# A wider slot table for the first experts, smaller last slot groups and evenly dealt scatters in a two-layer attention and experts kernel

## The reference: what is computed

```python
x = x + L0_xattn(layernorm(x), ctx, ...)   # 16 heads, masked by equal layer index
x = x + L0_ffn(layernorm(x))               # 8 experts, top 2 of each token, no capacity limit
x = x + L1_xattn(layernorm(x), ctx, ...)   # two-way attention and a gate
x = x + L1_ffn(layernorm(x))               # 8 experts, top 2, at most 640 tokens an expert

# L0_ffn
top_w, top_idx = top_k(softmax(xf @ router_w.T), 2)
combine = sum(one_hot(top_idx, E) * softmax(top_w)[..., None], axis=1)
out = einsum('te,ted->td', combine, silu(x @ w1[e]) @ w2[e] * scale[e])
# L1_ffn
seq = cumsum(expert_label, axis=0) * expert_label
valid = (seq > 0) & (seq <= capacity)
slot = seq - 1                            # where the token stands in its expert's buffer
out = (silu(disp @ W1) * (disp @ W2)) @ W3
```

## Time and profile before

| | |
|---|---|
| time, three runs | 1536.22 us median (1533.29 to 1537.31) |
| profiled execution | 1534.38 us, of it 1532.6 us from the first to the last instruction |
| PE busy | 1356.7 us (89%) |
| DVE, ACT, POOL busy | 847.2, 816.1, 671.5 us |
| mean granted TensorE clock | 0.955 of full speed |

### The profile page before, as it was taken

One profiled execution on the slowest core, in us unless ns is written; L12 is line 12 of the kernel. 1 busy time (PEld: TensorE's weight loads), 2 busy tenths in 40 slices (PEclk: granted clock), 3 DMA queues, 4 the chain that ended last, 5 costly groups with the idle time before them and its releaser, 6 DMA issues.

```text
span 1532.6 us, 37450 instructions
## 1 busy us (share of the span) xinstructions
PE 1356.7 (89%) x12922; PEld 1100.2 (72%) x12922; DVE 847.2 (55%) x2350; ACT 816.1 (53%) x1904; POOL 671.5 (44%) x935
## 2 busy tenths in 40 slices
PE   5999999997169999999996899999982999999996
PEld 4787777775136666667664888888871888888985
DVE  4787788776423222332231677777762566666663
ACT  3787778775035555554552555555541545454442
POOL 3234545454453333333302456666655344444322
PEclk8999999999579999999998999999995999999998
DMA  3333435442059999988885223332222333343331
GB/s 113 111 113 98 121 94 103 108 90 54 21 112 178 201 193 182 183 169 149 161 160 121 69 84 84 83 84 83 81 64 57 109 124 113 123 130 104 127 104 50
DMA packets 280856, 172.76 MB, mean 113 GB/s; under 512 B 212990, under 2 KB 259424, under 8 KB 280676
## 3 DMA queue, kind: packets, MB, share of 16 engines
q1 hardware_dynamic: 257940, 134.65, 38.8%
q0 software_dynamic: 18608, 32.14, 7.7%
q10 hardware_dynamic: 4128, 3.57, 0.8%
HBM read 93.40 MB, written 31.80 MB: 82 GB/s over the span
## 4 chain that ended last, share of the span: by engine, by line
PE 81%; issue 4%; ACT 4%; DVE 3%; DMA 3%; POOL 2%; another core or an unknown queue 1%; ACTq 0%; SPq 0%; DVEq 0%; POOLq 0%
PE psum L2285 14%; PE psum L1355 12%; PE psum L1342 11%; PE psum L2298 7%; PE psum L1822 4%; PE psum L1903 4%; PE psum L1828 3%; PE psum L747 2%; PE psum L805 2%; PE psum L734 2%; PE psum L708 2%; PE psum L822 2%; PE psum L1893 2%; PE psum L808 2%; PE psum L786 2%
## 5 line engine op out<-in xcount | busy, mean ns | idle before, releaser
L1273 DVE SCALAR_TENSOR_TENSOR b_h<-b_hid,b_h 128x1024 f16<-128x1024 f32 x71 | 87.0, 1225 | 280.6 <-ACT b_h L1305 274.7
L2285 PE MATMUL psum<-d_xT,d_w 128*128 128x256 f16 (+1 forms) x2304 | 231.5, 257 | 5.3 <-DVE d_xT L2374 2.9
L1342 PE MATMUL psum<-arena,b_xT 128*128 x852 | 200.2, 386 | 28.0 <-DMA b_xT<-b_x 27.6
L2285 PEld LDWEIGHTS psum<-d_xT,d_w 128*128 128x128 f16 x2304 | 200.1, 99 | 24.1 <-DVE d_xT L2374 2.5
L1355 PE MATMUL psum<-arena,b_hT 128*128 x1704 | 200.5, 274 | 13.9 <-DMA b_hT<-b_h 8.8
L1355 PEld LDWEIGHTS psum<-arena,b_hT 128*128 128x128 f16 x1704 | 166.0, 98 | 52.9 <-issue 20.2
L1342 PEld LDWEIGHTS psum<-arena,b_xT 128*128 128x128 f16 x852 | 84.3, 99 | 119.1 <-issue 36.6
L1300 ACT ACTIVATE b_hid<-psum 128x512 f32<-128x512 f32 x142 | 84.7, 597 | 136.3 <-PE psum L1342 85.6
L1183 POOL DMA_INDIRECT b_xg<-dram_normed,b_gi x71 | 67.1, 945 | 205.2 <-DVE b_x L1266 193.6
L2339 ACT ACTIVATE d_sg<-psum 128x256 f32<-128x256 f32 (+1 forms) x192 | 65.8, 348 | 147.7 <-PE psum L2285 136.3
L2384 DVE SCALAR_TENSOR_TENSOR d_hf<-psum,d_sg 128x256 f32<-128x256 f32 (+1 forms) x192 | 71.0, 379 | 107.8 <-ACT d_sg L2339 89.3
(11 more groups left out here) (316 smaller groups left out, 2930.4 us busy)
## 6 DMA issues: line engine op xcount, KB each, us to landing
d_wst<-in_L_w SPq DMA_DIRECT2D x64, 384.0 KB
stage<-in_L_w SPq DMA_DIRECT2D x32, 512.0 KB
dram_expert_rows<-b_ys SPq DMA_DIRECT2D x71, 128.0 KB
ctxT<-in_ctxT SPq DMA_DIRECT2D x64, 128.0 KB
dram_normed<-xn SPq DMA_DIRECT2D x64, 128.0 KB
x<-in_x SPq DMA_DIRECT2D x32, 128.0 KB, 5.8
dram_x<-xnew SPq DMA_DIRECT2D x32, 128.0 KB
c_x<-dram_x SPq DMA_DIRECT2D x32, 128.0 KB
```

The costliest lines, as they stand in the source:

```text
L1273: dve.scalar_tensor_tensor(out=h16[:, p, 1, :], in0=hid[:, p, :], scalar=H_SCALE, in1=h16[:, p, 0, :], op0=ALU.mult, op1=ALU.subtract).the ...
L1342: i = pe.matmul(psum[:, 1 + 2 * p + half, :], xT[:, j % NT, px, c, :], weights(e, c, pw, half * 512, 512), start=(n == 0), stop=(n == len( ...
L2285: i = pe.matmul(psum[:, q, m * n:(m + 1) * n], w16[:, fc % RING, pw, col:col + P], xT[:, p, px, c, at:at + n], start=(k == 0), stop=(k == ...
```

## The change

Two parts. First, the table `ids[0]` gets two words per slot, and each scatter of A writes the token's number twice (8 bytes from `pairs`, where it was 4 bytes from `tokens`); `load_ids` fetches both words, and `gather` uses the first. The fill of the table is twice as long. Second, in C the group of blocks 24 to 27 becomes two groups of two, the slot buffers get five places, and the scatters are dealt to POOL's turns by a list: at most three a turn, the first behind `norm2`, the second behind `norm1`, the third behind `gather`. The loop runs two turns longer, in place of a loop of scatters alone at the end.

```diff
-        ids = [dram_ids("ids0", SPARE0 + P, 1), dram_ids("ids1", SPARE1, 2)]
+        ids = [dram_ids("ids0", SPARE0 + P, 2), dram_ids("ids1", SPARE1, 2)]
...
+            pairs = sa("pairs", [P, NB, 2], I32)
...
-                for t, n in ((ids[0], SPARE0 + P), (ids[1], 2 * SPARE1)):
+                for t, n in ((ids[0], 2 * (SPARE0 + P)), (ids[1], 2 * SPARE1)):
...
-                pool.iota(no_token[:, :], pattern=[[0, (SPARE0 + P) // P]], base=T, channel_multiplier=0)
+                pool.iota(no_token[:, :], pattern=[[0, 2 * (SPARE0 + P) // P]], base=T, channel_multiplier=0)
...
+                pool.iota(pairs[:, :, :], pattern=[[P, NB], [0, 2]], base=0, channel_multiplier=1)
...
-                                            tokens[:, b:b + 1], None, bounds_check=bound, oob_is_err=False).then_inc(scat[g % 4], 16)
+                                            pairs[:, b, :], None, bounds_check=bound, oob_is_err=False).then_inc(scat[g % 4], 16)
...
-            gi = sa("gi", [P, NX, 1], I32)
+            gi = sa("gi", [P, NX, 2], I32)
...
-            RG = 4
+            RG, NS = 4, 5
...
-            GROUPS = [(b, RG) for b in range(0, NB - RG, RG)] + [(NB - 4, 2), (NB - 2, 1), (NB - 1, 1)]
+            GROUPS = [(b, RG) for b in range(0, NB - 2 * RG, RG)] + [(NB - 8, 2), (NB - 6, 2), (NB - 4, 2), (NB - 2, 1), (NB - 1, 1)]
...
-                def scatters(b):
-                    for g, (first, n) in enumerate(GROUPS):
-                        j = b - 4 - (first + n - 1)
-                        if 0 <= j < n:
-                            scatter(first + j)
+                turn = {}
+                at = 0
+                for b in range(NB):
+                    g, j, n = group_of[b]
+                    for k in range(2):
+                        at = max(at, b - j + n + 3)
+                        if len(turn.get(at, ())) == 3:
+                            at += 1
+                        turn.setdefault(at, []).append((b, k))
...
-                for b in range(NB + 2):
+                for b in range(NB + 4):
+                    s = turn.get(b, ())
                     norm2(b - 2)
-                    scatters(b)
+                    for c in s[0:1]:
+                        scatter(*c)
                     norm1(b + 2)
+                    for c in s[1:2]:
+                        scatter(*c)
                     gather(b + 3)
-                for b in range(NB + 2, NB + 5):
-                    scatters(b)
+                    for c in s[2:3]:
+                        scatter(*c)
...
-                    if due(g - 2):
-                        dve.wait_ge(scat[g % 3], scattered(g - 3))
+                    if due(g - NS + 1):
+                        dve.wait_ge(scat[g % NS], scattered(g - NS))
```

More of the change, by code:

```diff
@@ L200, in build @@
         brief = region(SHARED + WEIGHTS - 20480, 20480)
-        zrow, no_token = brief("zrow", [P, D]), brief("no_token", [P, (SPARE0 + P) // P], I32)
+        zrow, no_token = brief("zrow", [P, D]), brief("no_token", [P, 2 * (SPARE0 + P) // P], I32)
         x1, x2 = dram("x1", (T, D)), dram("x2", (T, D))
@@ L1447, in second_attention @@
             gslot = sa("gslot", [P, RG * 2])
[L1448 removed]
+            gsidx, gsidw = sa("gsidx", [P, NS, RG * 2], U32), sa("gsidw", [P, NS, RG * 2, 2], I32)
             c_const, c_cast = sem("c_const"), psem("c_cast")
@@ L1452, in second_attention @@
             yg_ld, x_ld, ctx_ld = load_sems("c_gather"), [sem(f"c_row{i}") for i in range(6)], load_sems("c_ctx")
-            xs_st, scat = load_sems("c_xs_st"), [sem(f"c_scat{i}") for i in range(3)]
+            xs_st, scat = load_sems("c_xs_st"), [sem(f"c_scat{i}") for i in range(NS)]
             x2_steps, x2_ready, n1_stat, n1_rstd, xn_ready, xt_done, xnT_ready = (psem(f"c_{n}") for n in (
@@ L1485, in scattered @@
             def scattered(g):
-                return sum(32 * GROUPS[i][1] for i in range(g + 1) if i % 3 == g % 3)
+                return sum(32 * GROUPS[i][1] for i in range(g + 1) if i % NS == g % NS)
             def nth(b, n=2):
@@ L1626, in c_sync @@
                     sp.wait_ge(xs_st[p], nth(NB - 2 + p))
-                for p in range(3):
-                    sp.wait_ge(scat[p], scattered(len(GROUPS) - 3 + (p - len(GROUPS)) % 3))
+                for p in range(NS):
+                    sp.wait_ge(scat[p], scattered(len(GROUPS) - NS + (p - len(GROUPS)) % NS))
             def c_pool(pool):
@@ L1664, in norm2, with scatter @@
                         pool.tensor_scalar(rstd2[:, p, 1:2], mv2[:, p, 0:1], rstd2[:, p, 0:1], -1.0, ALU.mult, ALU.mult).then_inc(n2_rstd, 1)
[L1666 to L1675, removed]
-                def scatters(b):
-                    for g, (first, n) in enumerate(GROUPS):
-                        j = b - 4 - (first + n - 1)
-                        if 0 <= j < n:
-                            scatter(first + j)
+                def scatter(b, k):
+                    g, j, n = group_of[b]
+                    if j == 0 and k == 0:
+                        pool.wait_ge(slot_ready, g + 1)
+                        pool.wait_ge(w_ready, g + 1)
+                    at = 2 * j + k
+                    pool.indirect_dma_start(ids[1], bass.IndirectOffsetOnAxis(ap=gsidx[:, g % NS, at:at + 1], axis=0),
+                                            gsidw[:, g % NS, at, :], None, bounds_check=bound, oob_is_err=False).then_inc(scat[g % NS], 16)
+                turn = {}
+                at = 0
+                for b in range(NB):
+                    g, j, n = group_of[b]
+                    for k in range(2):
[3 more added lines that the diff above has]
+                        turn.setdefault(at, []).append((b, k))
+                assert max(turn) == NB + 3
                 gather(0)
@@ L1698, in c_pool @@
                     pool.wait_ge(xs_st[p], nth(NB - 2 + p))
-                for p in range(3):
-                    pool.wait_ge(scat[p], scattered(len(GROUPS) - 3 + (p - len(GROUPS)) % 3))
+                for p in range(NS):
+                    pool.wait_ge(scat[p], scattered(len(GROUPS) - NS + (p - len(GROUPS)) % NS))
             def c_act(act):
@@ L2120, in slots_out @@
                     dve.wait_ge(slot_steps, m + 6)
-                    if due(g - 2):
-                        dve.wait_ge(scat[g % 3], scattered(g - 3))
-                    dve.tensor_copy(gsidx[:, g % 3, 0:2 * n], gslot[:, 0:2 * n]).then_inc(slot_ready, 1)
+                    if due(g - NS + 1):
+                        dve.wait_ge(scat[g % NS], scattered(g - NS))
+                    dve.tensor_copy(gsidx[:, g % NS, 0:2 * n], gslot[:, 0:2 * n]).then_inc(slot_ready, 1)
                 add_experts(0)
```

4 lines of the change are left out of this document (2 added, 2 removed).

## The result

The changed kernel takes 1538.80 us (median of 6 runs, 1536.84 to 1540.90), the kernel before on the same chip 1533.36 us (6 runs, 1527.17 to 1537.31). The ratio is 1.0042 with a 95% interval of 1.0025 to 1.0059: slower by 0.42% (the two medians alone give 1.0035, inside that interval). The forecast was 1525.5 us, faster. The profiled execution after has a span of 1536.8 us, against 1532.6 us before.

What follows compares the result with a forecast made beforehand. PE was taken as the bound inside the stages, and what each transition waits for last between them. Terms -8.3 - 5.7 + 1.5 + 1.2 + 0.6 = -10.7 us against the 1536.22 us median gave 1525.5 us, range 1518.5 to 1534.5.

Steps and rivals of the forecast that it cites:

- Part one: A to B: 8-byte slots land sooner after the last scatter, so B's loads and PE start 8.3 us earlier.
- Rival 1: A to B: the wait is not due to slot width, DVE may hold POOL's descriptors back; 1533.8 us, chance 0.12.
- Part two: End of C: eight scatters instead of twelve follow the last `norm2`, so D starts 5.7 us earlier.
- Part three (a): Inside C: one more group, of two blocks, costs 1.5 us.
- Part three (b): Inside C: three scatters a turn make `norm2` 1.15 us late, mostly covered by ACT's idle time; costs 1.2 us.
- The uncovered bound given: Inside C: cost of three scatters a turn if nothing covered the late `norm2`, 13.8 us.
- Part three (c): Inside C: gathers start later behind the second scatter, with 0.38 us of margin left; costs 0.6 us.
- rival 3: Inside C, DVE's L1981: gathers come late, each us beyond 3.24 costing 1 us a turn; 1550 us, chance 0.04.
- rival 2: Inside C: POOL becomes the pace, with the late `norm2` uncovered; 1538.1 us, chance 0.07.
- The sign that the prediction itself had named for rival 2: Inside C: four turns with a group should stay near 38.8 us; beyond 40.5 it is rival 2.
- The other sign: Inside C: PE's waits before L1932 would tell, with the starts of `norm2`, what three scatters a turn cost.
- Rival 4: Whole kernel: every added cost in C is hidden and the clock comes early; -17.5 us, 1518.7 us, chance 0.07.

Runs made afterwards that it cites:

- run 1: Kernel before with only stage A's table widened to 8 bytes a slot, stage C untouched; ratio 0.9952 to the kernel before.
- Run 8: Kernel before with stage A's scatters writing 4 bytes into slots 8 bytes apart, stage C as before; ratio 0.9960 to the kernel before.
- run 7: Kernel before with each token written four times into stage A slots of 16 bytes, stage C as before; ratio 0.9946 to the kernel before.
- run 3: Changed kernel with at most two scatters a turn up to turn 28, both behind `norm2` and ahead of `norm1`; ratio 0.9932 to the kernel before.
- run 6: run 3 with blocks 24 to 27 as one group again and up to four scatters in turns 31 and 32; ratio 0.9948 to the kernel before.
- run 4: Changed kernel with the gather issued ahead of the second and third scatter; ratio 0.9986 to the kernel before.
- run 10: Changed kernel with the second scatter back ahead of `norm1` and the third after the gather; ratio 0.9935 to the kernel before.
- run 5: Changed kernel with two scatters a turn up to turn 28, the second still between `norm1` and the gather; ratio 1.0070 to the kernel before.
- run 11: Changed kernel with a third buffer for gathered rows and every gather issued one turn earlier; ratio 1.0013 to the kernel before.
- run 2: Changed kernel with stage A's 4-byte table restored, leaving only stage C's part; ratio 1.0054 to the kernel before, 8.3 us slower.

## Why the prediction was wrong

**Part one (-8.3): right in kind, too large by a third, for a reason that was not the one given.** A-B fell by 6.0 us in the changed kernel and by 5.6 in run 1, whose time fell by 7.4. The prediction wrote that "the visible difference is in what is written: 4 bytes to a slot in A, 8 in C". Run 8 shows that width alone is not it: the distance between slots is. C's tail, also 8 bytes apart, lands in 2.76 us where A at 8 bytes needs 5.0 to 5.5 (4.4 and 4.8 in two later runs); why A needs 16 to get there stays open. Rival 1, DVE holding POOL's descriptors back, is out: in run 1 and after, the load starts earlier with DVE's work unchanged, in the changed kernel even before DVE has ended.

The rows, first, say 11.04, 5.45 and 2.90 us for slots of 4, 8 and 16 bytes. By the rule of the Trainium skill that the prediction cited ("DMA: Bandwidth & Descriptors", section Specifications: below 512 B a transfer reads, modifies and writes) all three are alike in kind, and the gain would be 0; the runs do not agree, and the measurement decides. The same page's section "Anatomy of one DMA — SWDGE (gpsimd) path" gives a fixed 2.0 us for one transfer however small; the 2.90 us of run 7 and the 2.17 of the earlier trace rows agree with such a floor. An estimate from that figure: beyond 16 bytes at most 0.9 us is left to gain.

**Part two (-5.7): right.** Eight scatters follow the last `norm2` back to back; 5.4 us were won.

**Part three (a), one more group (+1.5): too small.** It measured +2.5 (run 3) and 2.6 (run 6). The term was taken from a four-turn average; the cost falls into turns 28 to 30, one of them 12.02 us long.

**Part three (b), three scatters in a turn (+1.2): the step that failed.** The working was right up to its last sentence. It foresaw `norm1` waiting, POOL free at 10.4 us and `norm2` 1.15 us late; the trace has 10.59 and 1.4 to 1.8. Then it let ACT's idle 0.94 us a turn, before `c_th`, take the lateness up. Run 4 isolates this term, with the gathers on time: 7.0 us over run 3, 8.3 over run 10, not 1.2. In sum the cover took up nearly all of it: from 860 to 1120 us `norm2` is late by 13.9 us in all in run 4, and ACT's idle time before `c_th` fell by 13.3, from 23.4 to 10.1 us. C grew all the same, and not by the path that the prediction had looked at. It followed a late `norm2` only to `c_th`, `xn2T` and PE's L1932, and PE's wait there is 12.3 us in run 4 where it was 14.2. PE waits more for `normalise_x`, behind `norm1`, 7.1 us where it was 0.5, and 3.5 us for DVE's `c_pr`, which was no wait before. How the lateness gets from `norm2` to these two was not followed step by step. The uncovered bound given, 13.8, was not reached either: a group's four turns take 39.8 to 40.0 us in run 4 and 38.3 to 38.6 in run 3, so about one lateness a group is lost and not two. What the prediction did not see is that the 1.2 us come from emptying a wait: two scatters in the old place and the third at the end (run 10) leave `norm2` 0.3 to 0.5 us late.

**Part three (c), gathers later (+0.6): the second step that failed.** It compared one landing of 2.86 us, from the quiet start of C, with a margin of 0.38 us. Under load a gather takes 4.48 us from issue to DVE's add in the round of run 5 shown above. And it priced a late gather as a one-way delay, "each us of landing beyond 3.24 costs 1 us a turn", which is rival 3; but the gather, the add, the statistic and `norm1` form a loop, with a slack of 0.03 us in that round (9.21 against 9.24). By that price a landing of 4.48 us in about 20 turns would have cost some 25 us. It measured 5.4 us (run 4) to 6.2 (run 11), and 18.9 where all four turns of a group have a scatter in the loop (run 5); in the changed kernel the fourth turn has none and lets it recover.

The sum from the measured terms: -6.0 - 5.4 + 2.5 + 7.0 + 5.4 = +3.5 us; what is measured is +5.4 in the medians and +4.2 between the two profiled spans. The remainder is A, 1.6 us later, B, 2.4 longer from its first load to C's first `norm2`, and D, 3.4 shorter; between the runs here these stages vary by as much with no edit that aims at them.

So the case is rivals 2 and 3 together, each at a lower price than its own, and they had 0.11 between them: each was seen, each was dismissed by a cover of less than 1 us. The sign that the prediction itself had named for rival 2, four turns beyond 40.5 us, was there: 948.61 to 990.90 on the starts of `norm2` is 42.3. It took both to bring it about, as run 4, without the late gathers, stays at 40.0 us or less. The other sign, a longer wait of PE before L1932, was not there. Rival 4 is out: nothing was hidden, and the mean granted clock is the same.

## What to carry to other kernels

A short instruction that stands ahead of a wait may cost nothing, because it fills the wait; moved behind it, it costs its length and leaves the wait empty (here 1.28 us from start to start of a scatter, and 1.06 us of idle time before `norm1`). Before spreading work over a turn, mark where the engine waits in the turn as it is, and put the additions there. Look for the loop that runs through an engine and back (here gather, add, statistic, `norm1`, gather) and sum it: in this kernel an addition outside it cost next to nothing (run 10), one inside it was paid nearly every turn (run 5), and idle time elsewhere did not cover it. Follow a late operation along every path to the bounding engine, not only along the one that has a cover. And change the two ends of a stage without touching its steady state: both gains here were real, and runs 3 and 10 keep them.

## What the runs showed of the hardware

- How long a run of small indirect scatters takes to land depends on the distance between the slots in DRAM: from the last issue to B's first load it took 11.04 us at 4 bytes apart (10.42 in run 2), 5.93 at 8 apart with 4 bytes written, 4.40 to 5.46 at 8 apart with 8 written, 2.90 to 3.40 at 16 apart with 16 written. The table of C, 8 apart, landed within 2.8 us; why it is faster is open. POOL's own time for issuing the last one is the same, 0.97 us, in all of them.
- An indirect gather's rows took 3.5 to 6.2 us from issue to use inside C, where DVE waited for them in run 5 (4.48 in the round shown), and 2.86 from issue to landing at its start.
